# Zeroing transfers of an eight-core MoE layer with the groups of rows as first dimension and the experts as second

## What is computed

```python
mod = (_silu(L0_c) @ L0_wmod).reshape(4, 6, 1, -1)      # sa, ca, ga, sb, cb, gb
h = _layernorm(x) * (1 + ca) + sa
x = x + ga * ttt(h)             # K, V, Q = h @ theta.T; per token: g = 2/d*(W@k+b - v);
                                # W -= LR*outer(g, k); b -= LR*g; out = W@q + b
h = _layernorm(x) * (1 + cb) + sb
x = x + gb * (shared_ffn(h) + sum over the top 2 of 8 experts of score * expert_ffn(h))
```

## Time and profile before

| | us |
|---|---|
| median of 3 runs | 1697.76 (1693.86 to 1698.08) |
| profiled execution, its own time | 1702.7 |
| its span (slowest core, core 0) | 1700.8 |
| even cores 0, 2, 4, 6 | 1700.8, 1691.9, 1687.8, 1685.2 |
| odd cores 1, 3, 5, 7 | 1629.5, 1636.9, 1626.8, 1629.2 |
| PE busy on core 0 | 1386.9 (82%) |
| DVE, ACT, POOL busy on core 0 | 697.4, 394.3, 111.5 |

### The profile page before, as it was taken

The page is one execution under the profiler, slowest core; times in us unless marked ns, Lnnn a source line. Parts: engine busy times, 40 slices in busy tenths (PEclk is TensorE's granted clock), DMA queues, the critical chain, the costliest instruction groups (busy, mean ns, idle before and its releaser), DMA issues.

```text
span 1700.8 us, 22529 instructions; the slowest of 8 cores (1626.8 to 1700.8 us)
## 1 busy us (share of the span) xinstructions
PE 1386.9 (82%) x8207; PEld 758.8 (45%) x8207; DVE 697.4 (41%) x1173; ACT 394.3 (23%) x627; POOL 111.5 (7%) x119
## 2 busy tenths in 40 slices
PE   0578422661599899988979999999999999998997
PEld 0343210230244444455434446666666666543444
DVE  3446830140364565465433333222222222225775
ACT  1132210230244444344321112221122211010010
POOL 0000000000000100101110000000000000002330
PEclk9989766776799899999989999999999999998999
DMA  8964421121456445122939427489999998839562
GB/s 231 253 154 163 163 95 64 65 80 60 131 192 205 168 186 212 62 88 93 244 79 248 152 97 191 119 176 184 191 202 194 179 182 175 170 105 374 191 199 90
DMA packets 88475, 272.48 MB, mean 160 GB/s; under 512 B 7581, under 2 KB 7709, under 8 KB 81694
## 3 DMA queue, kind: packets, MB, share of 16 engines
q0 software_dynamic: 43568, 98.07, 30.6%
q1 hardware_dynamic: 34886, 124.55, 21.0%
q10 hardware_dynamic: 9896, 48.24, 7.7%
HBM read 277.14 MB, written 100.66 MB: 222 GB/s over the span
## 4 chain that ended last, share of the span: by engine, by line
PE 67%; DMA 8%; DVE 8%; issue 6%; ACTq 4%; another core or an unknown queue 3%; ACT 1%; POOL 1%; DVEq 0%; SPq 0%; POOLq 0%
PE u L911 10%; PE up L885 8%; PE gate L885 8%; PE prep L647 6%; PE gate L877 5%; PE up L877 5%; PE prep L911 5%; ACTq L986 4%; DMA xb<-x 3%; DMA ygb<-yx,sl 3%; PE u L809 2%; PE up L739 2%; PE gate L774 2%; PE up L774 2%
## 5 line engine op out<-in xcount | busy, mean ns | idle before, releaser
L1395 DVE TENSOR_TENSOR act<-up,sgb 128x640 bf16<-128x640 f32 x64 | 52.8, 825 | 224.9 <-PE up L885 224.9
L809 PE MATMUL u<-Gsb,Ktk 128*128 128x512 bf16 x256 | 70.8, 402 | 90.8 <-DVE WT L1268 90.7
L1065 ACT ACTIVATE sgb<-gate 128x512 bf16<-128x512 f32 (+1 forms) x80 | 44.4, 554 | 309.0 <-PE gate L877 302.8
L1392 DVE TENSOR_TENSOR act<-up,sgb 128x512 bf16<-128x512 f32 (+1 forms) x80 | 50.9, 637 | 149.2 <-PE up L877 140.9
L1067 ACT ACTIVATE sgb<-gate 128x640 bf16<-128x640 f32 x64 | 45.0, 703 | 250.6 <-PE gate L885 250.6
L647 PE MATMUL prep<-hft,s_thK 128*128 128x512 bf16 (+1 forms) x320 | 73.2, 382 | 35.3 <-ACT hft L976 31.5
L911 PE MATMUL u<-w1d,act 128*128 128x512 bf16 x408 | 95.2, 384 | 0.8 <-DVE tmpy L1403 0.8
L911 PE MATMUL u<-w0d,act 128*128 128x512 bf16 x408 | 95.1, 383 | 0.0
L1268 DVE TENSOR_TENSOR WT<-WT,u 128x512 f32<-128x512 f32 x128 | 81.7, 679 | 9.6 <-PE u L809 9.4
L1576 POOL DMA_INDIRECT hx<-h2m,sl x36 | 39.0, 1084 | 667.7 <-DVE sl L1375 378.1
L1035 ACT CAST Wbf<-WT 128x1024 bf16<-128x1024 f32 x64 | 66.4, 1038 | 61.2 <-issue 59.5
(11 more groups left out here) (238 smaller groups left out, 2340.7 us busy)
## 6 DMA issues: line engine op xcount, KB each, us to landing
hx<-zero ACTq DMA_DIRECT2D x4, 6656.0 KB
yx<-ring SPq DMA_DIRECT2D x40, 512.0 KB, 4.3
rowstg<-wmod SPq DMA_DIRECT2D x16, 1024.0 KB, 5.3
hx<-zero ACTq DMA_DIRECT2D x4, 2560.0 KB
hxb<-hx ACTq DMA_DIRECT2D x8, 1280.0 KB, 9.1
xb<-x SPq DMA_DIRECT2D x18, 512.0 KB, 6.2
x2b<-x SPq DMA_DIRECT2D x18, 512.0 KB, 6.4
x2s<-x2b SPq DMA_DIRECT2D x18, 512.0 KB, 6.8
```

What stands on the lines that cost most here:

```text
L809: m = t.matmul(U[jh][:, 0:512], Ktk[s % 2][:, cc * D + dt * P:cc * D + (dt + 1) * P], Gsb[:, cc * D + jh * 512:cc * D + (jh + 1) * 512], s ...
L1392: v.tensor_mul(act[k % 2][:, fj * ACW:fj * ACW + COLS[k]], R[2 + n % 2][:, 0:COLS[k]], sgb[n % 2][:, 0:COLS[k]]).then_inc(v_act, 1)
L1395: v.tensor_mul(ap(act[k % 2], fj * ACW, [[DT * ACW, P], [HC, 2], [1, HC]]), ap(up2, 0, [[1024, P], [512, 2], [1, HC]]), ap(sgb[n % 2], 0, ...
```

## The change

```diff
@@ -983,8 +983,8 @@
                         i = arg[0]
                         lo, step_, ne, n, done = ((2 * i * CAP, CAP, 2, CAP, hx_zeroed) if i < 4 else
                                                   (OVB + OVC * (i - 4), REG - CAP, NE, OVC, beyond_zeroed[i - 4]))
-                        s_.dma_start(ap(d_hx, lo * D, [[step_ * D, ne], [ZR * D, n // ZR], [1, ZR * D]]),
-                                     ap(d_zero, 0, [[0, ne], [0, n // ZR], [1, ZR * D]])).then_inc(done, 16)
+                        s_.dma_start(ap(d_hx, lo * D, [[ZR * D, n // ZR], [step_ * D, ne], [1, ZR * D]]),
+                                     ap(d_zero, 0, [[0, n // ZR], [0, ne], [1, ZR * D]])).then_inc(done, 16)
```

## The result

The changed kernel takes 1631.95 us (median of its runs, 1630.27 to 1639.02) against 1695.81 us (1691.18 to 1698.08), a ratio of 0.963 with a 95% interval of 0.960 to 0.966. In the second series, beside other kernels, it was 0.962 (0.961 to 0.963). The ratios compare only executions in the faster of two states, since in some executions the cores of one die, or of both, show a lower granted clock and take longer. The gain is 64 us. The forecast was 1615 with 1602 to 1632 as its band; the time lies in that band by 0.05 us, between the forecast and the first rival's 1639.

A forecast was written before the change was run, and what follows sets the result against it. The even cores bound the kernel at 1700.8 us, the odd cores next at 1636.9. Freed even cores reach about 1559, so the slowest odd core decides: 1636.9 - 23.4 = 1613.5, plus 1.9, 1615 us; range 1595 to 1643.

The forecast's parts named there:

- rival 1: Odd cores gain nothing, so the time stops at their present span: 1639 us; chance 0.21.
- Even cores' held issue, 88.1 us: ACT on core 0: three idle stretches behind slow issues of zeroing transfers, 29.80 + 40.99 + 17.28 us, go.
- scatter, 53.8 us: Core 0's first scatter no longer waits for the zeros: DVE's wait falls from 56.62 to 2.8 us.
- The bound passes to the odd cores: Once the even cores are faster, the odd cores set the time; their bound stands only 63.9 us below.
- Price of a packet: Engine time for 8 KB of zeros: 0.308 us, or 0.425 us beside much other traffic.
- The odd cores' waits for `xb`, 23.4 us: DVE's three waits for late `xb` loads on core 3, 17.3 us, go; times 1.35 the gain is 23.4 us.
- the factor between gain and waits: Odd cores' gain per us of `xb` wait removed: 1.35 taken, the middle, with 1.7 as upper case.
- Done well before the load: Odd cores' zeroing transfers take 5 or 12 us, ending before the `xb` load issued 25 us behind them.
- the first two places: Of three places where DVE on core 3 waits for `xb`, those with waits of 5.5 and 3.7 us.
- Rival 3: Slower: bursts of zeros on 16 engines delay the odd cores' `xb` loads by up to 95 us, 1734 us; chance 0.03.
- Expert part, counted at 0: Odd cores' weight loads when even cores arrive earlier: gain 0 to 10.9 us, loss about as possible, 0 counted.
- A queue of about 210 packets: ACT's held issues read as a queue holding some 200 to 213 waiting packets; at most 80 per engine after the change.

The follow-up runs named there:

- e5: Changed kernel with the early zeroing transfers of both roles on 4 engines, the late ones as changed; 1631.28 us, ratio 0.960 to the kernel before.
- e2: Kernel before with the new order of the zeroing transfers on the odd cores alone; 1705.2 us, ratio 1.007.
- e4: Changed kernel with the odd cores' zeroing pieces moved right behind an even step's first load; ratio 0.975, four runs from 1637.04 to 1656.57 us.
- e6: Changed kernel with the even cores' early transfers on 4 engines and their late ones in the old order; 1619.59 us, ratio 0.958.
- e10: Changed kernel with the even cores' early transfers on 8 engines and both roles' late ones in the old order; 1620.2 us, ratio 0.957.

## Why the prediction was right or wrong

The direction, the even cores and the change of the bound were right. That the time lies in the forecast's band is partly luck: the odd cores' gain of 23.4 us, which the 1615 rests on, did not come, and what happened is nearer to rival 1.

- *Even cores' held issue, 88.1 us, and scatter, 53.8 us: right.* Sum to 1559 us; core 0 came to 1564.9, the others to 1552 to 1558. Both mechanisms are shown, by the rows after and by e5, which brings back 20 us of each.
- *The bound passes to the odd cores, and only 64 us of the even cores' 136 are seen: right.*
- *Price of a packet: wrong.* I took 0.308 us on all 16 engines, with 0.425 as the worst. Measured: 0.431 on core 0, 0.430 to 0.463 on core 3 beside a quiet neighbour, 0.72 to 0.77 when both cores write zeros at once. My 0.308 came from two engines. Eight engines still gave it (0.478 x 16 x 16 us / 393 = 0.311), so no row of the kernel before showed what sixteen would do; only the neighbour's part was left out without a reason. For the even cores the fourth transfer took 14.9 us where 6.2 to 8.5 were forecast, and it still landed 3.4 us before the row numbers.
- *The odd cores' waits for `xb`, 23.4 us: this is the step that failed.* They went, from 18.3 to 4.1 us, in e2, where the even cores stayed as they were, and the first scatter came 13.6 us earlier for 14.2 us of waits: the factor between gain and waits is about 1.0, not the 1.35 that I took. In the changed kernel they stayed at 21.4 and 17.5 us. "Done well before the load" held for core 3's own transfers at the first two places, and the loads were late all the same, beside core 2's zeros; at the third it did not hold (34.3 us, not 12, and the load follows after some 23). The sum looked at one core at a time: neither it nor a rival had the even cores' new 16-engine bursts beside the odd cores' loads.
- *Rival 3, the burst in front of a load*, was given 3% as a slowdown. Its mechanism came true once per core (a load of 20.6 us on core 3, waits of 5.0 to 5.5 on the four), at a price that only offset a gain.
- *Rival 1* (odd cores gain nothing, 1639) describes the outcome best, and the profiled execution is at 1639.02. The reason given for it was that loads and zeros meet; they do, as e4, e6 and e10 confirm, but at two of the three places the zeros are another core's.
- *Expert part, counted at 0:* 668.9 to 663.5 us in both profiled executions of the changed kernel, a gain of 5.4. The last scatter came 6.0 us later in the first of them and 1.1 in the second, so only part of it is seen. The 7 us between rival 1 and the median are about what the slowest odd core of a run gains (6.1 and 9.5 us on average, 1637.1 to 1631.0 and 1627.6); where these arise beyond the expert part is not shown.
- *A queue of about 210 packets:* only an estimate, from the least that can have stood there. The count is 232 to 233 on two engines and 152 on four. Nothing in the sum hung on it but that 80 packets are few enough, which held.

## What to carry to other kernels

Look at the share of engines a transfer takes before its size: a first dimension of 2 put 10 MB on two engines, and the issuing engine's sequencer stood still with everything behind it. But the widest spread is not the best one when the transfer has time: give it enough engines to meet its date and leave the others to the loads that somebody waits for. When the slowest role is freed, the next bound is another role's, and it may depend on what its neighbour does: work out a transfer's cost with all cores' new times and widths, not one core at a time.

## What was not expected of the hardware

- Sixteen engines copying 8 KB packets from memory to memory gave 228 GB/s on core 0, and 272 to 284 GB/s on core 3 beside a core that writes few or no zeros, 13% to 41% above what eight gave (201), and 159 GB/s beside a core doing the same.
- Reading the same 8 KB from all engines costs nothing that shows: 0.722 against 0.724 us a packet.
- A core's loads are late with no zeros of its own in flight: 7.3 us beside 69% of 16 engines on core 2, 3.9 us where core 2 used two engines (e2).
- A transfer's handing over was held with 232 to 233 packets per engine standing on two engines and with 152 on four, and was not held with 94 on eight.
- The even cores' late transfers, 104 groups first, took 82.3% of 16 engines in 445 to 455 us on core 2, about 13 engines.
